# A graph layer's beginning rearranged: constants, tables and loads in a new order, four row gathers per block in one piece

## What is computed

```python
xs, xd = x[edge_src], x[edge_dst]                    # rows of both ends of each edge
r = edge_vec / norm(edge_vec);  sh1 = sqrt(3) * r    # direction of the edge
h1 = relu(emb @ fc1_w1 / sqrt(10)); w  = h1 @ fc1_w2 # weights that belong to the edge
h2 = relu(emb @ fc2_w1 / sqrt(10)); w2 = h2 @ fc2_w2
# s_t, v_t: bilinear in (xs, xd, sh1) and w;  scal, gates, vecs: bilinear in (s_t, v_t, sh1) and w2
edge_out = concat([tanh(scal), vecs * tanh(gates)]) * norm
x = layernorm(x + segment_sum(edge_out, edge_dst, num_segments=3125))
```

## Time and profile before

| | us |
|---|---|
| median of 3 runs | 744.84 (744.56 to 747.78) |
| the profiled execution | 744.64 |
| its span | 742.8 |
| PE busy | 687.2 (93%) |
| DVE busy | 691.7 (93%) |
| ACT busy | 560.2 (75%) |
| POOL busy | 528.0 (71%) |

### The profile page before, as it was taken

One profiled execution on the slowest core, in us unless ns is written; L12 is line 12 of the kernel. 1 busy time (PEld: TensorE's weight loads), 2 busy tenths in 40 slices (PEclk: granted clock), 3 DMA queues, 4 the chain that ended last, 5 costly groups with the idle time before them and its releaser, 6 DMA issues.

```text
span 742.8 us, 19328 instructions
## 1 busy us (share of the span) xinstructions
PE 687.2 (93%) x5990; PEld 282.9 (38%) x5990; DVE 691.7 (93%) x1231; ACT 560.2 (75%) x1281; POOL 528.0 (71%) x653
## 2 busy tenths in 40 slices
PE   2359999999999999999999999999999999999984
PEld 2113334434443444344344444334434443444321
DVE  7488999999999999999999999999999999999986
ACT  3238887887888778888888888877788888878752
POOL 5676888778876887688768886787778876887200
PEclk7569999999999999999999999999999999999998
DMA  5412211111111211121112111211121111111000
GB/s 132 112 34 47 47 32 28 40 46 28 30 42 27 50 26 42 28 47 31 43 26 45 29 43 27 48 31 27 40 46 29 28 39 26 41 27 27 20 1 23
DMA packets 45822, 28.49 MB, mean 38 GB/s; under 512 B 23299, under 2 KB 43941, under 8 KB 45721
## 3 DMA queue, kind: packets, MB, share of 16 engines
q1 hardware_dynamic: 31402, 19.43, 9.9%
q0 software_dynamic: 13312, 6.84, 6.0%
q10 hardware_dynamic: 1006, 0.96, 0.5%
HBM read 22.46 MB, written 4.74 MB: 37 GB/s over the span
## 4 chain that ended last, share of the span: by engine, by line
PE 87%; DVE 4%; issue 2%; ACT 1%; POOL 1%; DVEq 0%; ACTq 0%
PE ps L1073 16%; PE ps L986 14%; PE ps L1004 13%; PE ps L993 9%; PE ps L1053 8%; PE ps L974 6%; PE ps L1029 5%; PE ps L1066 4%; PE ps L1060 3%; PE ps L964 3%; PE ps L1041 3%; PE ps L948 2%; PE ps L1021 2%; DVE p_s L751 2%; ACT v_s L528 1%
## 5 line engine op out<-in xcount | busy, mean ns | idle before, releaser
L374 POOL DMA_INDIRECT xs<-in_xp,src_i x416 | 401.0, 964 | 115.2 <-issue 104.3
L751 DVE TENSOR_TENSOR p_s<-ps,h 128x2048 f32<-128x2048 f32 x104 | 238.3, 2292 | 21.6 <-PE ps L1073 20.9
L791 DVE TENSOR_TENSOR z_s<-ps,h 128x2048 f32<-128x2048 f32 x104 | 237.6, 2284 | 1.3 <-PE ps L1029 1.2
L528 ACT CAST v_s<-ps 128x512 bf16<-128x512 f32 x312 | 182.2, 584 | 48.3 <-PE ps L986 43.2
L1073 PE MATMUL ps<-f,w_f 32*128 32x512 f32 x832 | 119.7, 642 | 4.3
L986 PE MATMUL ps<-p_s,sum_m 128*32 128x512 f32 x832 | 111.7, 605 | 0.6 <-DVE p_s L751 0.5
L1004 PE MATMUL ps<-z_s,w_z 128*32 128x512 f32 x832 | 110.8, 605 | 1.5 <-DVE z_s L791 1.5
L494 ACT COPY f<-ps 128x512 f32<-128x512 f32 x104 | 61.0, 587 | 41.9 <-PE ps L974 41.5
L993 PE MATMUL ps<-v_s,less 128*128 128x512 bf16 x208 | 81.1, 390 | 2.8 <-ACT v_s L528 2.6
L416 POOL TENSOR_TENSOR along<-fe,r 128x192 f32<-128x192 f32 x104 | 54.2, 521 | 32.8 <-ACT fe L506 26.3
L1053 PEld LDWEIGHTS ps<-ident,u 128*128 128x128 f32 x416 | 43.8, 141 | 87.6 <-issue 87.0
(11 more groups left out here) (129 smaller groups left out, 848.7 us busy)
## 6 DMA issues: line engine op xcount, KB each, us to landing
emb<-e_dram SPq DMA_DIRECT2D x309, 30.0 KB
xs<-in_xp,src_i POOLq DMA_INDIRECT x416
e_dram<-e_part SPq DMA_DIRECT2D x7, 360.0 KB, 3.0
e_in<-in_emb SPq DMA_DIRECT2D x8, 240.0 KB, 2.9
window<-x_dram SPq DMA_DIRECT2D x104, 7.9 KB
eo_all<-in_vec_t SPq DMA_DIRECT2D x1, 528.0 KB, 5.0
x_dram<-eo_all SPq DMA_DIRECT2D x1, 525.0 KB
place<-place_dram SPq DMA_DIRECT2D x26, 20.0 KB
```

What stands on the lines that cost most here:

```text
L374: nc.gpsimd.indirect_dma_start(xs_r[n][:, t, :], None, xp, bass.IndirectOffsetOnAxis(src_i[:, m * T + t:m * T + t + 1], axis=0)).then_inc( ...
L528: nc.scalar.copy(v_s[:], v_ps).then_inc(v_step, 1)
L751: nc.vector.tensor_tensor(p_s[:], ps[:, 0:4, :], h1_r[m % 2][:].unsqueeze(1).to_broadcast([128, 4, BE]), ALU.mult).then_inc(p_done, 1)
L791: nc.vector.tensor_tensor(z_s[:], ps[:, 0:4, :], h2_r[k % 3][:].unsqueeze(1).to_broadcast([128, 4, BE]), ALU.mult).then_inc(z_done, 1)
```

## The change

- **Places and x.** VectorE makes `spread` first, while it waits for the destinations, then the place table. The third part of x is written by VectorE (`rest_of_x(1)`), no longer by a subtraction and a copy on ScalarE. The misfit count comes behind both.
- **Queues.** The first source indices are loaded by ScalarE's queue ahead of the destinations; the rest of `vec_t` (528 KB) goes from SyncE's queue to ScalarE's, issued behind x's second part. SyncE stores x before it loads the first places, and reads the bases of windows 0 to 2 before it waits for the stored x; the rest of the places is stored behind the windows.
- **emb of block 0.** It is used whole, in f32: four small loads (`e_whole`, `w_whole`), one f32 matmul each for hidden_1(0) and hidden_2(0). The store of the first group's parts moves from ScalarE's queue to SyncE's, and the loads of block 0's parts (L588) are gone. The rests of the first group are made by VectorE, not GpSimd.
- **Constants.** `w_first` is made in step -1, `rep_m` and `w_z` in step 0, `iota` and `centre` in step 3; the copy `dst_f` is gone. `acc` is cleared by ScalarE in four activations (scale 0) in the setup, not by VectorE. The second set of `r4`: step 0 of it at i = -1, then at i = 1, 2, 2, 2, 3, 3, 4 (before: -2, -2, 0, 0, 0, 1, 1, 1).
- **Gathers.** Ten gathers (blocks 0, 1 and half of 2) stand ahead of GpSimd's branch, four before. In the loop GpSimd gathers the four tiles of block i+4, then does directions(i+3). ScalarE copies sources(i+3) as the last thing in step i (from i = -1 on), before it was beside copy_rows(i+3).
- **Small things.** Two more warm-up pairs on TensorE, two at i = -2; TensorE reads the misfit count at i = -3, not -4; later groups of `emb` are split over steps 3, 4, 5, 6, 7 in place of 3, 4, 6.

```diff
@@ sync
-                base = sp.value_load(bases[0:1, m:m + 1], min_val=0, max_val=N - 1)
+                    base = sp.value_load(bases[0:1, m:m + 1], min_val=0, max_val=N - 1)
+                else:
+                    base = first_bases[m]
...
-            sp.dma_start(src_i[:, 0:TA], src_t[:, 0:TA]).then_inc(src_loaded, 16)
+            for n in range(2):
+                sp.dma_start(e_whole[32 * n:32 * n + HID], emb[0:WHOLE * HID].rearrange("(b h) e -> h b e", h=HID)
+                             ).then_inc(whole_loaded, 16)
+                sp.dma_start(w_whole[32 * n:32 * n + HID], w1[0:HID, n, :]).then_inc(whole_loaded, 16)
             load_super(0)
...
-            sp.wait_ge(place_stored, 16)
-            load_places(0)
             sp.wait_ge(x_part_ready, PARTS)
...
-            sp.dma_start(of_blocks[FIRST:NB], place_part[FIRST:NB]).then_inc(place_stored, 16)
+            sp.wait_ge(place_stored, 16)
+            load_places(0)
             sp.wait_ge(bases_loaded, 16)
+            first_bases = [sp.value_load(bases[0:1, m:m + 1], min_val=0, max_val=N - 1) for m in range(3)]
             sp.wait_ge(x_stored, 48)
             load_window(0)
             load_window(1)
-            sp.wait_ge(emb_zeroed, 1)
             load_window(2)
-            load_emb(1)
-            sp.dma_start(vt[:, TA:TILES, :], vec_t[:, TA:TILES, :]).then_inc(vect_rest_loaded, 16)
+            sp.dma_start(of_blocks[FIRST:NB], place_part[FIRST:NB]).then_inc(place_stored, 16)
+            sp.dma_start(w_z[:].rearrange("p n c -> p (n c)"), w2b).then_inc(w2b_loaded, 16)
             load_window(3)
...
+            store_super(0)
             sp.wait_ge(place_stored, 32)
             load_places(1)
+            sp.wait_ge(emb_zeroed, 1)
+            load_emb(1)
+            load_emb(2)
@@ gpsimd
-            gather(0, 0, 3)
-            rest_of_emb(0, 0)
-            gather(0, 3, T)
+            gather(0, 0, T)
+            gather(1, 0, T)
+            gather(2, 0, 2)
             pool.wait_ge(misfits_ready, 1)
             flag = pool.value_load(misfits[0:1, 0:1], min_val=0, max_val=EP)
...
             with pool.Else():
                 pool.sem_inc(rows_final, NB)
-                rest_of_emb(0, 1)
-                gather(1, 0, 2)
                 pool.wait_ge(r4_ready, 1)
                 for i in STEPS:
...
+                    if real(i + 4) and i >= 0:
+                        gather(i + 4, 0, T)
+                    if real(i + 3):
+                        directions(i + 3)
+                    if i == -2:
+                        gather(2, 2, T)
+                        gather(3, 0, 2)
+                    if i == -1:
+                        gather(3, 2, T)
+                    later_emb(i)
@@ scalar
+            act.dma_start(src_i[:, 0:TA], src_t[:, 0:TA]).then_inc(src_loaded, 16)
             act.dma_start(dst_row_i, dst_rows).then_inc(dst_rows_loaded, 16)
...
             part_of_x(1)
+            act.dma_start(vt[:, TA:TILES, :], vec_t[:, TA:TILES, :]).then_inc(vect_rest_loaded, 16)
             part_of_emb(0, 0)
-            part_of_x(2)
-            part_of_emb(0, 1)
+            act.wait_ge(pool_consts, 5)
+            clean = acc[:].rearrange("p (n c) -> p n c", c=128)
+            for first, end in ((0, 7), (7, 13), (13, 19), (19, 25)):
+                nc.scalar.activation(clean[:, first:end, :], ident[:].unsqueeze(1).to_broadcast([128, end - first, 128]), ACT.Copy,
+                                     scale=0.0).then_inc(acc_zeroed, 1)
...
-            act.wait_ge(e_part_ready, PARTS)
-            act.dma_start(e_dram[:, 0:SB * HID, :].rearrange("n r e -> r n e"), e_part[0:SB * HID]).then_inc(e_stored, 16)
             copy_oht(0)
-            act.wait_ge(emb_zeroed, 1)
-            act.wait_ge(e_stored, 16)
-            for first in (0, 32, 64):
-                act.dma_start(emb_r[0][first:first + PARTS * HID], e_dram[:, 0:HID, :]).then_inc(emb_loaded[0], 16)
...
-                if i == -1:
+                if i == 2:
                     act.wait_ge(n2_ready, 2)
                     nc.scalar.activation(nrm_t[:, TA:TILES], n2_t[:, TA:TILES], ACT.Sqrt).then_inc(norm_ready, 1)
-                if real(i + 3) and i < 2:
+                if real(i + 3) and i < -1:
                     copy_sources(i + 3)
+                if i == -3:
+                    part_of_emb(0, 1)
...
+                if real(i + 3) and i >= -1:
+                    copy_sources(i + 3)
                 later_emb(i)
@@ vector
+                if i == 0:
+                    repeat_constants()
                 if real(i + 2):
                     sum_along(i + 2)
+                if i == -1:
+                    first_weights()
+                    directions(0, TA, TILES).then_inc(r4_step, 1)
                 if i == 0:
+                    second_weights()
+                if i == 3:
                     late_constants()
 
-                for step, at_step in enumerate((-2, -2, 0, 0, 0, 1, 1, 1)):
+                for step, at_step in ((1, 1), (2, 2), (3, 2), (4, 2), (5, 3), (6, 3), (7, 4)):
@@ tensor
-                    keep_warm(12)
+                    keep_warm(14)
+                    hidden_1(0)
                     misfits_of_all()
```

More of the change, by code:

```diff
@@ L38 @@
 FIRST = 8
+WHOLE = 1
 STRIPES = ((0, 112), (112, P))
@@ L731, in _ @@
             nc.vector.tensor_scalar(less[0][:], ident[:], of_part[:, 1:2], -1.0, ALU.mult, ALU.mult).then_inc(rep_step, 1)
[L732 to L738 removed]
+            rest_of_emb(1)
@@ new lines, in _, with repeat_constants @@
+            c1, c2 = 0.25 / math.sqrt(32.0), 1.0 / 16.0
+            dve.wait_ge(w2a_loaded, 16)
+            link(nc.vector.tensor_scalar(w_f[:], w2a_s[:, 1, :], c1 * SQRT3, None, ALU.mult))
+            nc.vector.scalar_tensor_tensor(out=w_f[:], in0=w2a_s[:, 0, :], scalar=c1, in1=w_f[:], op0=ALU.mult,
+                                           op1=ALU.add).then_inc(weights_ready, 1)
+            def repeat_constants():
+                for g in range(4):
+                    link(nc.vector.tensor_scalar(sel_g[:, g, :], sel_w[:], of_group[:, g:g + 1], of_part[:, 0:1], ALU.mult, ALU.mult))
+                    nc.vector.tensor_copy(rep_m[:, g], sel_g[:, g, :].unsqueeze(1).to_broadcast([128, 16, 8])).then_inc(rep_step, 1)
@@ L1056, in hidden_1 @@
             def hidden_1(m):
-                pe.wait_ge(emb_loaded[m % 3], 48 * (m // 3 + 1))
+                if m < WHOLE:
+                    pe.wait_ge(whole_loaded, 64)
+                    nc.tensor.matmul(h1_ps, w_whole[0:HID], e_whole[0:HID, m, :], start=True, stop=True).then_inc(h1_done, 1)
+                    return
+                if m == WHOLE:
+                    pe.wait_ge(weights_ready, 3)
+                pe.wait_ge(emb_loaded[m % 3], 48 * ((m - WHOLE) // 3 + 1))
                 if m >= 3:
@@ L1065, in hidden_2 @@
                     pe.wait_ge(acc_done, m - 5)
+                if m < WHOLE:
+                    nc.tensor.matmul(h2_ps, w_whole[32:32 + HID], e_whole[32:32 + HID, m, :], start=True, stop=True
+                                     ).then_inc(h2_done, 1)
+                    return
                 nc.tensor.matmul(h2_ps, w_first[:, 1, :], emb_r[m % 3][:], start=True, stop=True).then_inc(h2_done, 1)
@@ L1110, in _ @@
                     spread_edges(i + 4)
+                if i == -3:
+                    pe.wait_ge(misfits_ready, 1)
+                    flag = pe.value_load(misfits[0:1, 0:1], min_val=0, max_val=EP)
                 if real(i + 3):
```

161 lines of the change are left out of this document (72 added, 89 removed).

## The result

The changed kernel takes 734.81 us (median of 4 runs, 733.48 to 736.15), the kernel before 745.34 in the same comparison: a ratio of 0.985, 95% interval 0.982 to 0.987. The forecast was 736.4. The profiled execution is the longest of the four, 736.15 us with a span of 734.3; before it was 744.64 and 742.8. So the two traces differ by 8.5 us and the medians of this comparison by 10.5.

What follows compares the result with a forecast made beforehand. TensorE, 99% busy, was taken to bound the steady part, so only the beginning could gain: -8.6 us before product 0, +0.3 to product 5, zero after. From 744.64 that gives 736.3, stated as 736.4; range 733.5 to 740.8.

Steps and rivals of the forecast that it cites:

- The gathers: GpSimd's setup: ten gathers from 5.6 to 20.4 us, 14.8 us, five of them slowed beside wide VectorE pieces.
- D: Rival: gathers held up, first one-hot and everything else wait for GpSimd; directions(0) at 26.6, launch 740.4 us; chance 9%.
- The branch: GpSimd behind the gathers: branch issued near 18.5, 4.1 us until the next instruction, directions(0) near 22.6.
- Places, windows and rows(0): Setup: first one-hot near 16, windows issued at 16.7 behind the store of x, rows(0) near 18.5.
- B: Rival: stored x binds beside vec_t's load, windows at 22, 738.4 us; sign: GpSimd waits for copied rows; chance 12%.
- VectorE's floor: Setup: VectorE's constants end at 21.1, so directions(0) can't usefully start before 20.1; launch then 733.9 us.
- The clearing on ScalarE: Setup: ScalarE clears acc from 11.5 us, taking 3.5 us, hidden by GpSimd's gathers.
- Directions(0) to product 0: Beginning: up to 6.4 us from directions(0) to product 0, so product 0 at 29.0, 8.6 us earlier.
- Products 0 to 5: First blocks: five intervals of 6.2, 7.5, 10.6, 7.6 and 7.85, together 39.75 us, 0.3 more than before.
- C: Rival: r4's steps in step 2 stop products 3 to 5 three us more, product 3 over 11 behind 2; 739.4; 12%.
- The steady blocks: Loop: late source copy, four gathers and re-split emb groups cost zero; 6.51 us a block stays.
- A: Rival: late source copy lengthens each block at ScalarE's v_s, up to 0.3 us x 98, 766 us; chance 7%.

Runs made afterwards that it cites:

- u_gather4: Changed kernel with only block 0's four gathers ahead of GpSimd's branch, the other six behind it; 1076.02 us in one launch, kernel before 977.08.
- u_vec_late: Changed kernel with the rest of vec_t issued by SyncE behind the first three windows, not by ScalarE; 1091.95 us, ratio 1.104 to the kernel before.
- h2_early: Changed kernel with hidden_2(0) moved into the setup; 734.75 us in one launch, kernel before 746.63.
- mid_again: Changed kernel with sources copied beside copy_rows from step 6, hidden_2(0) in the setup, r4's second set started at step 0; 967.49 us, ratio 0.990.
- u_copy_mid: Changed kernel with sources(i+3) copied beside copy_rows(i+3) again from step 6 on; 968.97 us, ratio 0.991 to the kernel before.
- after_again: The changed kernel itself, unedited, on a chip with late signals; median 1026.30 us (984 to 1080), kernel before 1005.94.
- r4_spread: Changed kernel with r4's second set at steps 0, 1, 2, 2, 3, 3, 4 and the square root at i = 0; 1043.91 us, one launch.
- u_emb_part: Changed kernel with ScalarE's later emb pieces ahead of copy_f, late source copy kept; 1061.38 us, ratio 1.085 to the kernel before.
- mid_h2_r4: The same kernel as mid_again, in another run; 998.46 us, ratio 0.991 to the kernel before.
- emb_first: The kernel of u_emb_part with the edits of h2_early, r4_spread and u_vec_late added; 1062.15 us, ratio 1.073 to the kernel before.
- b_whole: Kernel before the change with only block 0's emb used whole, in f32; 1001.24 us in one launch, beside 1005.94 for the kernel before.
- emb_part_b: The kernel of u_emb_part repeated on another chip; 1069.04 us, ratio 1.092 to the kernel before.

## Why the prediction was right, and where it wasn't

**The gathers (too long).** I put them from 5.6 to 20.4, 14.8 us, with five of ten lengthened beside wide VectorE pieces. They ran from 4.72 to 18.01, 13.3 us; only three took over 1.0 us (1.14, 1.20, 1.61), though VectorE was busy for 12.2 of the 13.3. D didn't come: nothing waited for the gathers.

**The branch (wrong term).** I had the branch at 18.5, held by the gathers in the queue, with 4.1 us of fetch behind it and directions(0) at 22.6. It was issued at 15.2, as soon as the misfit count had been read, with three gathers unfinished, and the fetch ended before the last of them did. Its price on the path was zero. u_gather4 shows the price without the cover, 3.3 us. The 4.1 us are no fixed price either: behind branches at 14.0, 15.2 and 15.4 (the kernel before, the changed one, u_gather4) the sequencer went on at 17.96, 17.95 and 17.92. The Trainium skill, page "Runtime: NRT & Kernel Launch", section "Instruction fetch mechanics", says that a taken branch to a page outside the fetched ones waits for a fetch; the traces of the kernel before and of u_gather4 agree. The trace of the changed kernel adds that the wait is one of the sequencer, with the queued gathers running through it.

**Places, windows and rows(0) (right times, partly another path).** The first places are spread at 15.83 (forecast: first one-hot near 16), the windows are issued at 16.46 (16.7), and rows(0) was forecast near 18.5 and came at 18.50. With GpSimd done at 18.0 it is rows(0) that ends last: directions(0) at 19.32, 3.3 us before my 22.6. But the 16.7 came from the store of x, and in the trace the windows wait for SyncE, which loads the places when they have landed (13.46) and then reads three bases (13.8 to 16.2); in u_vec_late, with x stored 0.3 us later and the places landed earlier, they go out at 15.73. And rows(0) hangs on the one-hots and on TensorE's read of the misfit count behind them, 0.8 us, which the change puts there and my path didn't have. B's sign in the trace is there, a wait for the copied rows, but neither its cause nor its price: the stored x was not what ended last. The sign was badly chosen, since any delay of rows(0) gives it. VectorE's floor was high too: I had its constants end at 21.1, they end at 19.53, so the floor for directions(0) was 18.5 and not 20.1. The clearing on ScalarE took 3.15 us, for 3.5.

**Directions(0) to product 0 (right).** 6.22 us for 6.4. Of the 3.5 us that product 0 came earlier than forecast (25.54 for 29.0), 3.3 are the start of directions(0) and 0.2 this stretch.

**Products 0 to 5 (right sum, sizes off).** Forecast 6.2, 7.5, 10.6, 7.6, 7.85, measured 8.33, 6.44, 9.62, 7.60, 7.30. The first is the mis-sized one: I counted first_layer(1) behind sum_1(0) and left out the f32 matmul of hidden_2(0), 2.07 us on TensorE at half clock; h2_early moves it and takes 1.6 us away, 0.6 of them by an earlier rise of the clock. Product 2 did not wait for gathers, since they were done. Product 3 waits for the square root, 0.88 us idle and then the reciprocal, as forecast, and stays under the 11 us that C needed.

**The steady blocks (wrong).** "Later groups of emb: same pieces, one step apart, zero" is the step that failed, and with it the weighing of A. I looked at a block without emb, in which the 0.30 us of the copy is hidden, and took it for all; "hidden_2's copy there is released by TensorE anyway" isn't so where a piece of emb stands before it. In 15 blocks ScalarE has copy, piece of emb and hidden_2 in a row, and TensorE waits 0.21 to 0.28 us. It is A's mechanism in 15 of 98 blocks, at `over_nodes` and not at v_s where A looked: 2.1 us net. This is read from two traces on two chips and from the rows of the wait, which is there in these blocks alone. No run that takes the copy away was had on such a chip. So the cause is argued and not shown by an edit, and the rival of mid_again's text, that the work for emb at its new steps is enough without the late copy, is not ruled out by a run.

**The end (not in the sum).** I gave the tail nothing, since its code is untouched. Its clock isn't: 0.69 in 11 us of it, 1.7 us. The traces of the runs bear this out by the granted clock from 9 to 20 us behind product 103: the end took 29.2 to 29.7 us where it is 0.69 (h2_early, u_copy_mid, u_vec_late, u_gather4, after_again, r4_spread) and 27.5 to 27.8 where it is 1.00 (u_emb_part, mid_h2_r4, mid_again, emb_first); b_whole has 0.84 and 28.1, emb_part_b 0.57 and 32.0. The order of the code isn't what decides: u_emb_part and emb_part_b are the same kernel. What does stays open.

The time is therefore right in part by luck. The errors on the path (gathers and branch, 3.3 us too late) and the small ones behind it (0.2 and 0.5), 4.0 us in all, were given back by two terms that I had put at zero (2.1 and 1.7).

## What to carry to other kernels

- Work queued on GpSimd ahead of a branch runs while the sequencer fetches, and while it waits for the branch's value. Six gathers moved there were worth 7.2 us at product 0.
- To judge a piece moved into a loop, look for the fullest block of its period, not for a typical one. By the traces a copy of 0.30 us was free in 83 blocks and cost about 0.23 in the 15 in which another piece stands next to it.
- When several limits lie within two or three us of each other at the beginning, name the second and the third. Removing the first (b_whole: 4.7 us at directions) gave only 3.6 at the product. And don't take the releaser that a profile names for the bound when another piece ends within 0.1 us of it: the same row in the traces of other runs tells which it was.

## What the runs showed of the hardware

**A store beside a large load.** The store of the places took 3.77 us to land with 528 KB in flight on another queue (3.46 in h2_early, 3.71 in mid_again), 2.0 before and 2.1 in u_vec_late and emb_first. Loading them back then took longer in the last two, so that 0.1 to 0.25 us were left of it.

**Late signals behind TensorE's matmuls on three of five chips.** Here is VectorE in emb_first:

```profile
162.51 2.29 DVE L766 TENSOR_TENSOR p_s<-ps,h 128x2048 f32<-128x2048 f32 x1 [3.18 <-remote]
```

and TensorE in the same stretch, first_layer, whose end releases that product:

```profile
158.73 1.14 PE L1109 MATMUL ps<-f,w_f 32*128 32x512 f32 x8
159.69 0.38 PE L971 MATMUL ps<-place,spread 5*126 5x512 bf16 x1
161.41 0.39 PE L1017 MATMUL ps<-v_s,less 128*128 128x512 bf16 x1 [1.34 <-ACT v_s L524]
```

First_layer ends at 159.87 by its row, and the product starts 2.64 us later. In the traces of the first chip no product starts more than 0.08 us behind that end when VectorE waits for it; on the chips with late signals it is up to 4.0 us in the steady part (r4_spread, product at 462.75), more than the 3.4 that the expectations name. TensorE idles meanwhile, waiting for ScalarE. Between 100 and 500 us ScalarE idles for more than 1.2 us at a time 72 times in emb_first, 53 times in mid_again and not once in the changed kernel on the first chip. The granted clock from 120 to 680 us was 0.84 there, 0.92 in mid_again, and 1.00 on the first chip:

```profile
120.00:680.00 560.00, 425.43 (x3130) 169.69 (x3126) 353.67 (x605) 286.32 (x667) 274.71 (x340) 0.84 0.11 23
```

```profile
120.00:680.00 560.00, 455.66 (x3592) 173.57 (x3592) 407.59 (x694) 326.17 (x767) 312.88 (x388) 0.92 0.12 26
```

Ends of matmuls are modelled in these records, so the rows can't tell a late signal from a matmul that really took longer, and not whether the lower clock is cause or consequence. What they do tell is that the order of ScalarE's work, which goes with 0.2 us in some blocks on one chip, goes with 7 to 10% in four edited kernels (u_emb_part, emb_part_b, u_vec_late, emb_first) on others, where after_again is unclear. The gain of 1.5% is a statement about the first chip, and for one launch about chip E; for the chips with late signals after_again, from 2% faster to 7% slower, shows none.
